# Feed forward's table preparation as single VectorE operations between attention's own, and the attention output copied ahead of the next tokens

## The chip, the cores and the metric

One core of a Trainium2 chip runs the program. The metric is the device time of one execution in microseconds (us); three executions were timed before the change, and one more was profiled.

## The reference, cut to what matters

Two layers on x (16 batches of 64 tokens of 512) with a context of the same shape. The change touches the end of the first layer's attention and the start of its feed forward:

```python
x = x + L0_xattn(_layernorm(x), ctx, Wq, Wk, Wv, Wo, q_norm_w, k_norm_w)   # 32 heads, 8 kv heads of 128
x = x + L0_ffn(_layernorm(x), gate_*, up_*, down_*)                        # 4 bit weights, inner size 1376
x = x + L1_xattn(ctx, _layernorm(x), ctx)
x = x + L1_ffn(_layernorm(x), W_org, lora_down, lora_up, lora_keys, Wq)

def _dequant(qweight, scales, qzeros, g_idx):
    w = (qw[:, None, :] >> shifts & 15).reshape(-1, N)
    z = ((qz[:, :, None] >> shifts & 15) + 1).reshape(groups, -1)
    return (w - z[g_idx]) * scales[g_idx]
h = silu(xf @ Wg) * (xf @ Wu);  out = h @ Wd
```

## The kernel before

**Attention** is cut into 64 units: 8 kv heads times 8 pairs of batches. The program of each engine is written out by hand as steps j = 0 to 67 (`pe_step0`, `act_step0`, `dve_step0`, `pool_step0`), and a step holds different stages of up to five units. On TensorE (PE), step j holds the query projection of unit j (L366), the transposes of unit j-1's normed queries and keys (L392, L395), the key and value projection of unit j (L378), the scores of unit j-1 (L406), the transposes of unit j-2's probabilities (L413), the output projection of unit j-3 (L423) and unit j-2's probabilities times values (L433). Every fp32 product is made of three with the operands split into a high part (copied by ScalarE, ACT) and a low part (subtracted by VectorE, DVE).

DVE's step has a fixed order: low part of unit j-3's attention output (`aoT`, L557), the sum of unit j-4's output into `acc` (L562), low part of unit j-1's values (`vv`, L566), then of unit j the sum of squares of the queries (L571), `msq` (L573), and, when GpSimd (POOL) has raised it to the power -0.5 (`rms`, L662), the normed queries (`qn`, L576). The same for the keys follows (L580, L582, POOL L665, L596), with unit j-1's score maximum (L586) and unit j-2's low part of the transposed probabilities (L590) between them, and at the end unit j-1's softmax division (L601, L603). PE's key and value projection of step j waits for `vv` of unit j-1, because both use the same PSUM bank.

**Feed forward's preparation** hangs behind the steps: after step j each engine runs `pe_ahead(j)`, `act_ahead(j)`, `dve_ahead(j)` or `pool_ahead(j)`, which do something from step 57 on (n = j - 56 in the code). DVE there takes the 4 bit zero points apart (L1046, 16 instructions behind steps 57 and 58), writes the zero table (L1058, behind step 59), and makes the one-hot tables of the group indices (`one_hot`, L1028 to L1034, behind steps 60 to 63), then the layer norm's statistics and tokens (L673 to L677, L685). ACT and POOL split the scale table into three bf16 parts (ACT L956 behind steps 57 to 62, POOL L763 behind steps 58 to 61). `spread` (PE, L848 and L853) multiplies one-hot by table, and `dequant` (DVE, L1096 to L1106) makes a piece of weights of it, which ACT (`w_hi`, L978) and POOL (`w_lo`, L776) split. `x2_hi` (ACT, L971) and `x2_lo` (DVE, L1164) split the transposed tokens (PE L933). The first product of feed forward is L874. SP's queue issues the loads, each in order behind its waits. No scheduler changes any of this: the engines run what the code has in the order it has, and wait on semaphores.

Of the kernel before, what the change touches and what calls it, by code (L numbers as in the profile page):

```python
# [17 lines left out]
ALU = mybir.AluOpType  # L18
# [40 lines left out]
def block_kernel(nc, a, out, stop=None):  # L59
# [27 lines left out]
    with root:  # L87
# [295 lines left out]
        def pe_step0(st):  # L383
# [15 lines left out]
            if st.has(1, UNITS):  # L399
# [111 lines left out]
        def act_step0(st):  # L511
            act = nc.scalar
            if st.has(3, UNITS):
# [3 lines left out]
                               ACT.Copy).then_inc(s_aohi, 1)  # L517
            if st.has(1, UNITS):
# [34 lines left out]
        def dve_step0(st):  # L553
# [9 lines left out]
            if st.has(1, UNITS):  # L563
# [3 lines left out]
                                  vv[:, par, HI, :, :].bitcast(F32), ALU.subtract).then_inc(s_vlo, 1)  # L567
            if st.has(0, UNITS):
# [4 lines left out]
                dve.tensor_scalar(msq[:, 0:4], ssq[:, 0:4], 1.0 / HD, RMS_EPS, ALU.mult, ALU.add).then_inc(s_qms, 1)  # L573
                dve.wait_ge(s_rq, st.done(0))
# [147 lines left out]
        def sp_ffn(sp):  # L722
# [8 lines left out]
            sp.wait_ge(s_zero_v, 18)  # L731
# [79 lines left out]
        def pe_ahead(j):  # L811
            pe = nc.tensor
            n = j - UNITS
            if n == 0:
# [4 lines left out]
                pe.wait_ge(s_idx_v, 8)  # L819
                pe.wait_ge(s_scale_v, 6)  # L820
                pe.wait_ge(s_zero_v, 18)
                pe.wait_ge(s_qn, UNITS)
                pe.wait_ge(s_vlo, UNITS)
                spread(pe, 0, (0, 1))
# [117 lines left out]
        def act_ahead(j):  # L942
# [76 lines left out]
        def one_hot(dve, part):  # L1019
# [3 lines left out]
                           (slice(2 * D, 2 * D + F), GD, oh_d[:, :]))[part // 2]  # L1023
            raw, n = idx_raw[:, cols], idx_n[:, 0:cols.stop - cols.start]
            if part:
                dve.wait_ge(s_idx_v, 2 * part)
            if part % 2 == 0:
                dve.tensor_scalar(n, raw, 0.0, float(g), ALU.is_lt, ALU.mult).then_inc(s_idx_v, 1)  # L1028
                dve.wait_ge(s_idx_v, 2 * part + 1)
                dve.tensor_tensor(n, raw, n, ALU.add).then_inc(s_idx_v, 1)  # L1030
            else:
                dve.tensor_scalar(n, n, float(g - 1), 0.0, ALU.min, ALU.max).then_inc(s_idx_v, 1)
                dve.wait_ge(s_idx_v, 2 * part + 1)
# [3 lines left out]

        def dve_ahead(j):
            dve = nc.vector
            n = j - EVEN_DONE  # L1040
            if n == 1 or n == 2:
                if n == 1:
                    dve.wait_ge(s_zraw, 48)
                for k in range(4 * (n - 1), 4 * n):
                    for g, lo, hi in ZERO_TABLES:
                        dve.tensor_scalar(z_int[0:g, lo // 8:hi // 8, k], z_raw[0:g, lo // 8:hi // 8], 4 * k, 15,  # L1046
                                          ALU.logical_shift_right, ALU.bitwise_and).then_inc(s_zero_v, 1)
            if n == 2:
                dve.wait_ge(s_pid, 1)
                dve.tensor_scalar(shift[:, :], pid[:, :], 7, 2, ALU.bitwise_and, ALU.logical_shift_left).then_inc(s_col, 1)  # L1050
                dve.tensor_scalar(grp_i[:, :], pid[:, :], 31, None, ALU.bitwise_and).then_inc(s_col, 1)
                dve.wait_ge(s_col, 2)
                dve.tensor_copy(grp[:, :], grp_i[:, :]).then_inc(s_col, 1)
            if n == 3:
                dve.wait_ge(s_zero_v, 16)
                dve.wait_ge(s_zero, 2)
                for g, lo, hi in ZERO_TABLES:
# [945 lines left out]
```

## Time and profile before

| | us |
|---|---|
| median of three executions | 1195.75 |
| lowest and highest | 1193.85 and 1198.1 |
| profiled execution | 1194.14 |
| its span, first to last instruction | 1192.3 |
| PE busy | 1124.5 (94% of the span) |
| DVE busy | 753.9 (63%) |
| ACT busy | 542.5 (46%) |
| POOL busy | 416.8 (35%) |

Times in a view are microseconds from the span's start. An engine's idle time before an instruction is given with what ended it: `[2.08 <-DVE vv L566]`. A timeline's row gives the start, the duration, the engine, the line, what is written and read, and how many instructions it stands for. An instruction's duration reaches a little into the next one of its engine, so the distance from start to start is shorter than the duration.

### The profile page before, as it was taken

Reading aid. Unit: us, or ns where it says so; the run is one execution under the profiler, and the core shown is the slowest. Engines: PE = TensorE matmul, PEld = TensorE weight load, DVE = VectorE, ACT = ScalarE, POOL = GpSimd, SP = SyncE. Lnnn points to the kernel's source line nnn. Section 1 sums busy time; section 2 is a strip of 40 time slices with the busy share of each in tenths; the row PEclk is TensorE's granted clock in tenths of the full one; section 3 lists DMA queues with packets and bytes.
Section 4 is the critical chain, followed back from the end, with each engine's and each line's share of the span. In section 5 each row is a group of like instructions: output and inputs, shape, how many; then the busy total and the mean of one; then the engine's idle time right before and its main releaser. Section 6 shows DMA issues by size and latency. Waiting matters only on the chain. (4 is left out here: it accounts for less than half of the span.)

```text
span 1192.3 us, 19230 instructions
## 1 busy us (share of the span) xinstructions
PE 1124.5 (94%) x6643; PEld 961.4 (81%) x6643; DVE 753.9 (63%) x1572; ACT 542.5 (46%) x1437; POOL 416.8 (35%) x421
## 2 busy tenths in 40 slices
PE   4899999999999999999999988799999999798998
PEld 3799999899899899999989887567777777676776
DVE  6555555555555555555555777889864666687863
ACT  4444454554544544544444545333323445454531
POOL 4443323323332232332332433144422324554531
PEclk9999999999999999999999999989999999898999
DMA  6211011111101101101100110122202245133300
GB/s 211 76 36 32 23 37 32 29 32 31 35 25 32 37 23 32 36 24 31 37 23 4 40 30 1 27 72 80 76 26 54 62 107 124 44 77 74 89 2 36
DMA packets 48716, 56.49 MB, mean 47 GB/s; under 512 B 10822, under 2 KB 29270, under 8 KB 48620
## 3 DMA queue, kind: packets, MB, share of 16 engines
q1 hardware_dynamic: 48620, 55.26, 17.2%
q8 instruction: 54, 0.88, 0.3%
q14 instruction: 42, 0.34, 0.1%
HBM read 40.56 MB, written 2.10 MB: 36 GB/s over the span
## 5 line engine op out<-in xcount | busy, mean ns | idle before, releaser
L378 PE MATMUL bank<-wqkv,kvT 128*128 128x256 f32 x1536 | 199.8, 286 | 8.7 <-DVE vv L566 8.7
L423 PE MATMUL bank<-wo,aoT 128*128 128x512 f32 x768 | 192.0, 399 | 5.7 <-DVE acc L562 5.7
L378 PEld LDWEIGHTS bank<-wqkv,kvT 128*128 128x128 f32 x1536 | 188.0, 192 | 10.4 <-DVE vv L566 10.4
L366 PE MATMUL bank<-wqkv,kvT 128*128 128x512 f32 x768 | 188.5, 395 | 1.7 <-DVE qn L576 1.7
L423 PEld LDWEIGHTS bank<-wo,aoT 128*128 128x128 f32 x768 | 139.5, 188 | 33.4 <-DVE aoT L557 6.3
L366 PEld LDWEIGHTS bank<-wqkv,kvT 128*128 128x128 f32 x768 | 141.5, 190 | 28.8 <-issue 1.8
L662 POOL TENSOR_TENSOR rms<-msq,half_neg 128x4 f32<-128x4 f32 x64 | 64.5, 1008 | 220.4 <-DVE msq L573 220.2
L874 PE MATMUL bank<-x2T,wgu 128*128 128x512 f32 (+1 forms) x336 | 91.5, 416 | 0.0
L549 ACT ACTIVATE prob<-bank,nmax 128x128 f32<-128x128 f32 x256 | 90.3, 372 | 2.1 <-DVE nmax L586 2.1
L1905 POOL TENSOR_TENSOR pr<-pr,rc 128x512 f32<-128x512 f32 x64 | 66.7, 1045 | 69.6 <-DVE rc L1774 69.5
L665 POOL TENSOR_TENSOR rms<-msq,half_neg 128x2 f32<-128x2 f32 x64 | 44.6, 697 | 132.0 <-DVE msq L582 132.0
L576 DVE TENSOR_TENSOR qn<-bank,rms 128x512 f32<-128x512 f32 x64 | 44.3, 692 | 71.7 <-POOL rms L662 71.7
L527 ACT ACTIVATE qsq<-bank 128x512 f32<-128x512 f32 x64 | 38.2, 597 | 112.8 <-PE bank L366 112.8
L557 DVE TENSOR_TENSOR aoT<-bank,aoT 128x512 fp32r<-128x512 f32 x64 | 44.2, 691 | 65.7 <-ACT aoT L516 65.7
L538 ACT ACTIVATE ksq<-bank 128x256 f32<-128x256 f32 x64 | 24.6, 384 | 131.8 <-PE bank L378 131.8
L571 DVE TENSOR_REDUCE ssq<-qsq 128x4 f32<-128x512 f32 x64 | 44.0, 687 | 63.9 <-ACT qsq L527 63.8
L470 POOL TENSOR_TENSOR wqkv<-wqkv_raw,wqkv 128x768 fp32r<-128x768 f32 x28 | 51.8, 1851 | 62.6 <-ACT wqkv L457 62.6
L874 PEld LDWEIGHTS bank<-x2T,wgu 128*128 128x128 f32 (+1 forms) x336 | 62.1, 192 | 13.3
L406 PE MATMUL bank<-kT,qT 128*128 128x128 f32 x512 | 67.6, 275 | 1.2 <-ACT qT L531 1.2
L895 PE MATMUL bank<-wd,hT 128*128 128x512 f32 (+1 forms) x264 | 68.6, 405 | 0.0
L543 ACT ACTIVATE pT<-bank 128x512 fp32r<-128x512 f32 x64 | 38.3, 599 | 60.4 <-PE bank L413 60.4
L1661 ACT ACTIVATE pmT<-bank 128x512 fp32r<-128x512 f32 x64 | 38.2, 597 | 59.5 <-PE bank L1440 59.3
(176 smaller groups left out, 2207.0 us busy)
## 6 DMA issues: line engine op xcount, KB each, us to landing
wqkv_raw<-in_L_xattn_Wq_dram SPq DMA_DIRECT2D x32, 256.0 KB, 2.5
wo_raw<-in_L_xattn_Wo_dram SPq DMA_DIRECT2D x32, 256.0 KB, 2.6
qS<-qhl SPq DMA_DIRECT2D x32, 256.0 KB, 3.7
kS<-chl SPq DMA_DIRECT2D x32, 128.0 KB, 3.0
packed<-_L_ffn_gate_qweight_dram SPq DMA_DIRECT2D x40, 64.0 KB, 2.4
packed<-in_L_ffn_up_qweight_dram SPq DMA_DIRECT2D x40, 64.0 KB, 2.3
packed<-_L_ffn_down_qweight_dram SPq DMA_DIRECT2D x10, 256.0 KB
acc<-in_x_dram SPq DMA_DIRECT2D x8, 256.0 KB, 5.7
```

The costliest lines, as they stand in the source:

```text
L366: mm = pe.matmul(b_q[:, :], kvT[:, l, kt, p, 1:3, :], wqkv[:, par, r, kt, 0:QW], start=(kt == 0 and n == 0), stop=(kt == KT - 1 and n == 2))
L378: mm = pe.matmul(b_kv[:, b * 256:(b + 1) * 256], kvT[:, l, kt, p, 2 * b:2 * b + 2, :], wqkv[:, par, r, kt, QW:QKV], start=(kt == 0 and n = ...
L406: mm = pe.matmul(b_s[:, n * P:(n + 1) * P], qT[:, b, 2 * hp:2 * hp + 2, :], kT[:, b, :], start=True, stop=True)
L423: mm = pe.matmul(b_o[:, :], aoT[:, l, h, :, :], wo[:, par, r, h, :], start=(h == 0 and n == 0), stop=(h == G - 1 and n == 2))
L470: pool.tensor_tensor(wqkv[:, par, LO, n, :], wqkv_raw[:, n % 2, :], wqkv[:, par, HI, n, :].bitcast(F32), ALU.subtract).then_inc(s_wqkv, 1)
L549: act.activation(prob[:, n, :], b_s[:, n * P:(n + 1) * P], ACT.Exp, bias=nmax[:, n:n + 1], accum_out=psum_row[:, n:n + 1]).then_inc(s_exp, 1)
L576: dve.tensor_tensor(qn[:, :, :], b_q[:, :].rearrange("p (h d) -> p h d", h=G), rms[:, 0:4].unsqueeze(2).to_broadcast([P, G, HD]), ALU.mult ...
L662: pool.tensor_tensor(rms[:, 0:4], msq[:, 0:4], half_neg[:, 0:4], ALU.pow).then_inc(s_rq, 1)
L665: pool.tensor_tensor(rms[:, 4:6], msq[:, 4:6], half_neg[:, 4:6], ALU.pow).then_inc(s_rk, 1)
L874: mm = pe.matmul(b[0:w, :], wgu[:, f, l, m, kt, 0:w], x2T[:, r, kt, :], start=(kt == 0 and k == 0), stop=(kt == KT - 1 and k == 2))
L895: mm = pe.matmul(f_d[t][:, :], hT[0:w, l, t * P:(t + 1) * P], wd[0:w, f, r, :], start=(f == 0 and k == 0), stop=(f == FT - 1 and k == 2))
L1905: pool.tensor_tensor(pr[:, t % PT_, :], pr[:, t % PT_, :], rc1[:, t % 4:t % 4 + 1].to_broadcast([P, D]), ALU.mult).then_inc(s_n1, 1)
```

## The change

Every DVE piece of the table preparation that stood behind a step becomes single operations at three places of a step: "q" (behind `vv`, ahead of the queries' sum of squares), "rq" (behind `msq`, ahead of `qn`, while POOL makes `rms`) and "end" (behind the step, as before, but with one piece and not all). The zero table is written in three instructions and not two, so the semaphore's count is 19. The first `spread` moves on PE from behind step 64 into it. ACT's copies of the feed forward's tokens move from behind steps 64 and 65 to behind the `aoT` copy of steps 65 and 66. DVE makes the first two pieces of weights behind step 64 and not behind step 65, and ahead of the `x2_lo` of the first two token tiles.

```diff
@@ pe_step0, behind the scores
+            if st.j == UNITS:
+                pe.wait_ge(s_idx_v, 8)
+                pe.wait_ge(s_scale_v, 6)
+                pe.wait_ge(s_zero_v, 19)
+                pe.wait_ge(s_qn, UNITS)
+                pe.wait_ge(s_vlo, UNITS)
+                spread(pe, 0, (0, 1))
@@ act_step0, behind the aoT copy
+            act_tokens2(act, st.j - UNITS)
@@ dve_step0
+            dve_between(dve, st.j, "q")
             if st.has(0, UNITS):
...
                 dve.tensor_scalar(msq[:, 0:4], ssq[:, 0:4], 1.0 / HD, RMS_EPS, ALU.mult, ALU.add).then_inc(s_qms, 1)
+                dve_between(dve, st.j, "rq")
                 dve.wait_ge(s_rq, st.done(0))
@@ sp_ffn
-            sp.wait_ge(s_zero_v, 18)
+            sp.wait_ge(s_zero_v, 19)
@@ pe_ahead, n == 0
-                pe.wait_ge(s_idx_v, 8)
...
-                spread(pe, 0, (0, 1))
@@ act_ahead
-            if n == 8:
-                x2_hi(act, 0)
-                x2_hi(act, 1)
             if n == 9:
-                x2_hi(act, 2)
-                x2_hi(act, 3)
                 w_hi(act, 0, (0, 1))
+        def act_tokens2(act, n):
+            if n == 1 or n == 2:
+                x2_hi(act, 2 * n - 2)
+                x2_hi(act, 2 * n - 1)
@@ dve_ahead
+        BETWEEN = {(1, "q"): (0,), (1, "rq"): (1,), (1, "end"): (2,),
+                   (2, "q"): (3,), (2, "rq"): (4,), (2, "end"): (5,),
+                   (3, "q"): (6,), (3, "rq"): (7,), (3, "end"): ("columns",),
+                   (4, "q"): ("gate",), (4, "rq"): ("up",), (4, "end"): ("down",)}
+        HOT = {(5, "q"): (0,), (5, "rq"): (1,), (5, "end"): (2,),
+               (6, "q"): (3,), (6, "rq"): (4,), (6, "end"): (5,),
+               (7, "q"): (6,), (7, "rq"): (7,)}
...
-            if n == 9 or n == 10:
-                for p in (2 * (n - 9), 2 * (n - 9) + 1):
+            if n == 8:
+                dequant(dve, 0, (0, 1))
+            if n == 9:
+                for p in (0, 1):
                     dve.wait_ge(s_x2hi, p + 1)
                     x2_lo(dve, p)
-            if n == 9 or n == 10:
-                dequant(dve, 0, (2 * (n - 9), 2 * (n - 9) + 1))
+            if n == 10:
+                for p in (2, 3):
+                    dve.wait_ge(s_x2hi, p + 1)
+                    x2_lo(dve, p)
+                dequant(dve, 0, (2, 3))
```

Number k in the first table is a nibble position (two instructions, L1046 before), in the second one of the eight one-hot operations: 0 to 3 make `oh_gu` (1024 columns), 4 to 7 `oh_d` (1376 columns).

DVE from step 60's last operation to step 62's first, before the change; `idx_n` and `oh_gu` are the one-hot work:

```order
L603 TENSOR_TENSOR prob<-prob,rsum 128x512
L1028 TENSOR_SCALAR idx_n<-idx_raw 128x1024
L1030 TENSOR_TENSOR idx_n<-idx_raw,idx_n 128x1024
L673 BN_STATS stat<-acc 128x6
L675 BN_AGGR mv<-stat 128x2
L677 TENSOR_SCALAR mv<-mv 128x1
L557 TENSOR_TENSOR aoT<-bank,aoT 128x512
L562 TENSOR_TENSOR acc<-bank,acc 128x512
L566 TENSOR_TENSOR vv<-bank,vv 128x256
L571 TENSOR_REDUCE ssq<-qsq 128x4
L573 TENSOR_SCALAR msq<-ssq 128x4
L576 TENSOR_TENSOR qn<-bank,rms 128x512
```

and now (the lines have moved: L565 is before's L557, L586 its L576, L1032 its L1028):

```order
L613 TENSOR_TENSOR prob<-prob,rsum 128x512
L1061 TENSOR_SCALAR zs<-z_int 10x512
L683 BN_STATS stat<-acc 128x6
L685 BN_AGGR mv<-stat 128x2
L687 TENSOR_SCALAR mv<-mv 128x1
L565 TENSOR_TENSOR aoT<-bank,aoT 128x512
L570 TENSOR_TENSOR acc<-bank,acc 128x512
L574 TENSOR_TENSOR vv<-bank,vv 128x256
L1032 TENSOR_SCALAR idx_n<-idx_raw 128x1024
L580 TENSOR_REDUCE ssq<-qsq 128x4
L582 TENSOR_SCALAR msq<-ssq 128x4
L1034 TENSOR_TENSOR idx_n<-idx_raw,idx_n 128x1024
```

Two one-hot operations have left the stretch between `prob` and `aoT` for the two places around the sum of squares; the last part of the zero table has come into it.

ACT from step 64's exponentials to the first copies of weights, before:

```order
L549 ACTIVATE prob,psum_row<-bank,nmax 128x128 x3
L971 ACTIVATE x2T<-bank 128x4x128 [waits s_tx2] x2
L516 ACTIVATE aoT<-bank 128x512 [waits s_o,s_pv]
L543 ACTIVATE pT<-bank 128x512 [waits s_pv,s_pt]
L971 ACTIVATE x2T<-bank 128x4x128 [waits s_tx2] x2
L978 ACTIVATE wgu<-wtmp 128x256 [waits s_wt] x2
L516 ACTIVATE aoT<-bank 128x512 [waits s_o,s_pv]
```

and now:

```order
L557 ACTIVATE prob,psum_row<-bank,nmax 128x128 x3
L523 ACTIVATE aoT<-bank 128x512 [waits s_o,s_pv]
L975 ACTIVATE x2T<-bank 128x4x128 [waits s_tx2] x2
L551 ACTIVATE pT<-bank 128x512 [waits s_pv,s_pt]
L982 ACTIVATE wgu<-wtmp 128x256 [waits s_wt] x2
L523 ACTIVATE aoT<-bank 128x512 [waits s_o,s_pv]
L975 ACTIVATE x2T<-bank 128x4x128 [waits s_tx2] x2
```

Both copies of the attention output (`aoT`) have passed the pair of token copies (`x2T`) that stood ahead of them.

DVE in the same steps, from step 64's `prob` to step 65's `acc`, now:

```order
L613 TENSOR_TENSOR prob<-prob,rsum 128x512 [waits s_rec]
L1127 TENSOR_SCALAR nib<-packed,shift 128x256 [waits s_packed0]
L1133 TENSOR_TENSOR wint<-nib,bank 128x256 [waits s_zs,s_nib]
L1137 TENSOR_TENSOR wtmp<-wint,bank 128x256 [waits s_nib]
L1127 TENSOR_SCALAR nib<-packed,shift 128x256 [waits s_nib]
L1133 TENSOR_TENSOR wint<-nib,bank 128x256 [waits s_wt,s_zs,s_nib]
L1137 TENSOR_TENSOR wtmp<-wint,bank 128x256 [waits s_nib]
L683 BN_STATS stat<-acc 128x6 [waits s_acc]
L685 BN_AGGR mv<-stat 128x2 [waits s_bn]
L687 TENSOR_SCALAR mv<-mv 128x1 [waits s_bn]
L565 TENSOR_TENSOR aoT<-bank,aoT 128x512 [waits s_aohi]
L570 TENSOR_TENSOR acc<-bank,acc 128x512 [waits s_o]
```

The six instructions of `dequant` (L1127 to L1137) stood a step later before, behind `x2_lo`; now they are ahead of step 65's `aoT`.

## Rows read from the trace of the kernel before

**Rows 1.** Windows by step, 57 and 59 to 63: width, then busy time of each engine

```profile
656.44:667.52 11.08, 11.08 (x75) 10.04 (x74) 6.60 (x14) 5.33 (x16) 2.38 (x3) 1.00 0.01 1
...
679.96:692.43 12.47, 11.34 (x74) 10.06 (x73) 9.49 (x25) 6.24 (x17) 5.14 (x5) 1.00 0.30 100
692.43:704.82 12.39, 11.35 (x75) 10.07 (x74) 9.43 (x16) 6.49 (x17) 5.13 (x5) 1.00 0.24 64
704.82:718.24 13.42, 11.34 (x75) 10.06 (x74) 10.37 (x19) 6.48 (x17) 5.14 (x5) 1.00 0.01 1
718.24:731.18 12.94, 11.34 (x74) 10.06 (x73) 9.88 (x20) 6.48 (x17) 4.06 (x5) 1.00 0.01 2
731.18:744.09 12.91, 11.35 (x74) 10.07 (x73) 9.85 (x20) 5.24 (x16) 2.23 (x3) 1.00 0.00 0
```

**Rows 2.** Timeline of PE: the key and value projection of steps 57 and 61

```profile
659.76 3.12 PE L378 MATMUL bank<-wqkv,kvT 128*128 128x256 f32 x24
...
710.47 3.13 PE L378 MATMUL bank<-wqkv,kvT 128*128 128x256 f32 x24 [2.08 <-DVE vv L566]
```

**Rows 3.** Timeline of DVE: the idle places in step 57

```profile
660.02 0.69 DVE L571 TENSOR_REDUCE ssq<-qsq 128x4 f32<-128x512 f32 x1 [1.13 <-ACT qsq L527]
...
662.03 0.69 DVE L576 TENSOR_TENSOR qn<-bank,rms 128x512 f32<-128x512 f32 x1 [1.12 <-POOL rms L662]
663.33 0.42 DVE L580 TENSOR_REDUCE ssq<-ksq 128x2 f32<-128x256 f32 x1 [0.61 <-ACT ksq L538]
```

**Rows 4.** Timelines of POOL, then DVE: the end of step 60, the start of 61

```profile
702.00 3.46 POOL L763 TENSOR_TENSOR s_raw<-s_raw,zs 128x816 f32<-128x816 f32 x2
...
703.79 2.22 DVE L603 TENSOR_TENSOR prob<-prob,rsum 128x512 f32<-128x512 f32 x1
705.94 0.68 DVE L1028 TENSOR_SCALAR idx_n<-idx_raw 128x1024 f32<-128x1024 int32 x1
...
707.79 0.69 DVE L673 BATCH_NORM_STATS2 stat<-acc 128x6 f32<-128x512 f32 x1
...
708.80 0.68 DVE L557 TENSOR_TENSOR aoT<-bank,aoT 128x512 fp32r<-128x512 f32 x1
```

**Rows 5.** Timelines of ACT and DVE: the start of step 58

```profile
668.42 1.57 ACT L956 ACTIVATE zs<-s_raw 128x1632 bf16<-128x1632 f32 x1 [1.66 <-issue]
...
670.50 0.69 DVE L557 TENSOR_TENSOR aoT<-bank,aoT 128x512 fp32r<-128x512 f32 x1 [0.46 <-ACT aoT L516]
```

**Rows 6.** Table work: two lines' durations (ns, least/median/most), one row of the timeline

```profile
L1030 DVE TENSOR_TENSOR idx_n<-idx_raw,idx_n x2: 1226/1410/1593, 706.6 to 731.7; 128x1024 f32<-128x1024 int32 x1, 128x1376 f32<-128x1376 int32 x1
...
681.08 1.75 DVE L1046 TENSOR_SCALAR z_int<-z_raw 4x344 int32<-4x344 int32 x8
...
L1058 DVE TENSOR_SCALAR zs<-z_int x2: 408/991/1574, 693.5 to 695.0; 4x2752 bf16<-4x2752 int32 x1, 10x512 bf16<-10x512 int32 x1
```

**Rows 7.** A POOL power beside a DVE operation, and that line's durations (ns)

```profile
8.81 0.54 DVE L685 TENSOR_SCALAR xn<-acc,mv,rstd 128x512 f32<-128x512 f32 x1
...
8.97 0.79 POOL L681 TENSOR_TENSOR rstd<-mv,half_neg 128x1 f32<-128x1 f32 x1 [2.59 <-DVE mv L677]
...
L681 POOL TENSOR_TENSOR rstd<-mv,half_neg x24: 543/552/1235, 5.8 to 1167.9; 128x1 f32<-128x1 f32 x24
```

**Rows 8.** Timeline of all engines, steps 65 and 66

```profile
754.12 0.69 DVE L557 TENSOR_TENSOR aoT<-bank,aoT 128x512 fp32r<-128x512 f32 x1 [1.53 <-ACT aoT L516]
...
758.03 0.34 DVE L1096 TENSOR_SCALAR nib<-packed,shift 128x256 int32<-128x256 int32 x1
...
758.38 0.87 PE L433 MATMUL bank<-pT,vv 128*128 128x256 f32 x6
...
760.38 0.69 DVE L673 BATCH_NORM_STATS2 stat<-acc 128x6 f32<-128x512 f32 x1
...
761.31 0.60 ACT L516 ACTIVATE aoT<-bank 128x512 fp32r<-128x512 f32 x1
...
763.38 2.98 PE L423 MATMUL bank<-wo,aoT 128*128 128x512 f32 x12 [3.25 <-DVE acc L562]
```

More of the change, by code:

```diff
@@ L1017, in hidden_hi, with one_hot @@
             act.activation(hT[0:w, HI, :], hval[0:w, :], ACT.Copy).then_inc(s_hhi, 1)
[L1019 removed]
+        def one_hot(dve, k):
             cols, g, to = ((slice(0, 2 * D), GG, oh_gu[:, :, :].rearrange("p m k -> p (m k)")),
[L1023 removed]
+                           (slice(2 * D, 2 * D + F), GD, oh_d[:, :]))[k // 4]
             raw, n = idx_raw[:, cols], idx_n[:, 0:cols.stop - cols.start]
[L1025 to L1027 removed]
+            if k:
+                dve.wait_ge(s_idx_v, k)
+            if k % 4 == 0:
@@ L1034, in one_hot, with zero_bits @@
                 dve.tensor_scalar(to, n, grp[:, 0:1], None, ALU.is_equal).then_inc(s_idx_v, 1)
         ZERO_TABLES = ((GG, GATE, UP + F), (GD, DOWN, DOWN + D))
+        def zero_bits(dve, k):
+            if k == 0:
+                dve.wait_ge(s_zraw, 48)
+            for g, lo, hi in ZERO_TABLES:
+                dve.tensor_scalar(z_int[0:g, lo // 8:hi // 8, k], z_raw[0:g, lo // 8:hi // 8], 4 * k, 15,
+                                  ALU.logical_shift_right, ALU.bitwise_and).then_inc(s_zero_v, 1)
@@ new lines, in columns, with zero_table @@
+        def columns(dve):
+            dve.wait_ge(s_pid, 1)
+            dve.tensor_scalar(shift[:, :], pid[:, :], 7, 2, ALU.bitwise_and, ALU.logical_shift_left).then_inc(s_col, 1)
+            dve.tensor_scalar(grp_i[:, :], pid[:, :], 31, None, ALU.bitwise_and).then_inc(s_col, 1)
+            dve.wait_ge(s_col, 2)
+            dve.tensor_copy(grp[:, :], grp_i[:, :]).then_inc(s_col, 1)
+        def zero_table(dve, k):
+            if k == 0:
+                dve.wait_ge(s_zero_v, 16)
+                dve.wait_ge(s_zero, 2)
+            g, lo, hi = ((GG, GATE, UP), (GG, UP, UP + F), (GD, DOWN, DOWN + D))[k]
+            dve.tensor_scalar(zs[0:g, 0, lo:hi], z_int[0:g, lo // 8:hi // 8, :].rearrange("p c j -> p (c j)"), 1, None,
+                              ALU.add).then_inc(s_zero_v, 1)
@@ new lines, in block_kernel, with dve_between @@
+        BETWEEN = {(1, "q"): (0,), (1, "rq"): (1,), (1, "end"): (2,),
[3 rows of a table added]
+        HOT = {(5, "q"): (0,), (5, "rq"): (1,), (5, "end"): (2,),
+               (6, "q"): (3,), (6, "rq"): (4,), (6, "end"): (5,),
+               (7, "q"): (6,), (7, "rq"): (7,)}
+        def dve_between(dve, j, where):
+            n = j - EVEN_DONE
+            for k in BETWEEN.get((n, where), ()):
+                if k == "columns":
+                    columns(dve)
+                elif k in ("gate", "up", "down"):
+                    zero_table(dve, ("gate", "up", "down").index(k))
+                else:
+                    zero_bits(dve, k)
+            for k in HOT.get((n, where), ()):
+                if k == 0:
+                    dve.wait_ge(s_col, 3)
+                    dve.wait_ge(s_idx, 48)
+                one_hot(dve, k)
@@ L1040, in dve_ahead @@
             n = j - EVEN_DONE
[L1041 to L1057, printed above, removed]
-                    dve.tensor_scalar(zs[0:g, 0, lo:hi], z_int[0:g, lo // 8:hi // 8, :].rearrange("p c j -> p (c j)"), 1, None,
-                                      ALU.add).then_inc(s_zero_v, 1)
-            if n == 4:
-                dve.wait_ge(s_col, 3)
-                dve.wait_ge(s_idx, 48)
-            if 4 <= n <= 7:
-                one_hot(dve, n - 4)
+            dve_between(dve, j, "end")
             if n == 6 or n == 7:
-                dve.wait_ge(s_zero_v, 18)
+                dve.wait_ge(s_zero_v, 19)
                 ln_apply(dve, X2, n - 6, xn2[:, n - 6, :])
```

10 lines of the change are left out of this document (3 added, 7 removed).

## The prediction

> **What bounds the kernel now.** First the windows cut at the starts of the query projection, one per step [rows 1]: the first number is the step's width, then comes each engine's busy time. Step 57, the last in which DVE does attention's work alone, takes 11.08 us and PE is busy through all of it, so attention is bound by PE. Steps 59 to 63 take 12.47, 12.39, 13.42, 12.94 and 12.91 with the same PE work: 1.39, 1.31, 2.34, 1.86 and 1.83 us too long, 8.73 in all. Next the idle time of PE inside such a step: it is all in one place, ahead of the key and value projection, and ended by DVE's `vv` [rows 2]. Undisturbed, that projection starts 3.32 after the step (659.76 less 656.44).
>
> DVE's last four rows around a step's boundary tell why [rows 4]. Behind `prob` stand the table operations and the statistics, and only then `aoT`, which opens the next step. From `aoT` to PE's projection it takes 710.47 less 708.80, 1.67. So `aoT` may start 1.65 after the step's start (3.32 less 1.67) and PE loses nothing; in step 61 it started 3.98 after it (708.80 less 704.82), which gives the loss of 2.33.
>
> The same DVE sits idle elsewhere in a step [rows 3]: 1.13 ahead of the queries' sum of squares, 1.12 ahead of `qn` while POOL makes `rms`, 0.61 ahead of the keys' sum. The change moves work from the boundary, where it costs, to the first two of these.
>
> **Step 58 stays as it is.** It has a stall too, but there DVE waited for ACT's `aoT` copy [rows 5], and that stood behind ACT's 1.57 us `zs` copy, which did not start before 668.42. Nothing of that is moved: saved 0.
>
> **Steps 59 and 60.** At the end of steps 58 to 61 POOL subtracts in the scale table for 3.46 us, and `prob`, which has no more elements than DVE's 0.69 us rows [rows 3], takes 2.22 because it is held until POOL's second instruction ends [rows 4]. The operation behind it then starts 1.12 after the next step's start (705.94 less 704.82). The change leaves that hold alone. Eight nibble instructions took 1.75 [rows 6], so a pair takes 0.44. Behind step 58 one pair is left: `aoT` at 1.56, below 1.65. Behind step 59 three one-column instructions are left, estimated at no more than a pair. Both stalls go: 1.39 and 1.31 saved. The margin is 0.09; what is late next, if it doesn't hold, is PE's projection by as much as the pair is longer. The pairs at "q" and "rq" (0.44 each) are covered by the idle 1.13 and 1.12; without that cover they would cost 0.44 each.
>
> **Step 61.** In step 60 the two gate and up tables stand at "q" and "rq", each half of the 1.57 us instruction [rows 6], some 0.8; both fit their idle places. At the end are left the down table (0.41, 0.34 from start to start) and the statistics (707.79 to 708.80, 1.01). `aoT` starts at 1.12 + 0.34 + 1.01 = 2.47, PE's projection at 4.14, a stall of 0.82 in place of 2.34: 1.52 saved.
>
> **Step 62.** Left at step 61's end are one one-hot operation, as long as L1028 (0.68, taken as 0.71 with the step to the next), and the statistics: `aoT` at 2.84, a stall of 1.19. But step 61 itself is now full. `aoT` stands at 2.47, the sum of squares could follow 1.54 later (just before `vv` ends), "q" adds 0.71, and "rq" holds L1030, 1.23 us, all SBUF to SBUF. Beside what POOL does that matters. The nearest row is a power that began 0.16 behind a DVE operation of 0.54 and took 0.79, where the line's median is 0.55 [rows 7]: 0.24 longer, with the DVE operation 0.38 into it. So POOL loses the overlap less 0.14. For L1030 that is 1.07 less 0.14, 0.93. The bounds are 0 and the whole 1.07; I take 0.93, by the row. Then `qn` starts 2.01 behind the sum (662.03 less 660.02) plus 0.93, and the keys' sum 0.69 behind that: 2.47 + 1.54 + 0.71 + 2.01 + 0.93 + 0.69 = 8.35. PE's projection lets it start at 4.14 + 3.57 (663.33 less 659.76) = 7.71. It is 0.64 late, POOL's keys' power and its 3.46 us of subtractions are 0.64 late with it, and so is the release of `prob`. The stall becomes 1.19 + 0.64 = 1.83: 0.03 saved, 0.67 if nothing is late.
>
> The Trainium skill (SBUF: State Buffer, Who interferes with whom) says that DVE and GpSimd share one port pair, and that whichever comes first holds it for its whole instruction. By that rule the power would lose all of 1.07, and the sum below would be 0.14 smaller; the row has 0.24 where the rule has 0.38, so I stay with the row.
>
> **Step 63.** POOL subtracts nothing behind step 62. One operation on 1376 columns leaves that boundary (0.68 times 1376/1024, estimated at 0.91), L1030's long form (1.59) stays. Step 62 is full in the same way, but its "rq" operation is shorter, and by the same working some 0.1 late. 0.8 saved of 1.83.
>
> **Steps 64 to 66.** Here three moves meet [rows 8]. (a) Two one-hot operations leave the end of step 63; what PE needs next waits mostly for ACT, so I count only some 0.4 of earlier work in DVE's step 64. (b) Two pieces of weights, 758.03 to 760.38, 2.35 us, now stand ahead of step 65's `aoT`. That one was idle for 1.53 before 754.12 (for ACT's copy), so DVE was free at 752.59; with 2.35 more and 0.4 less it starts at 754.5, 0.4 later than before, and the output projection with it. Bounds: 0.8 later, or not at all. (c) ACT's copy of the last unit's `aoT` no longer waits behind two token copies and two weight copies. It was made at 761.31 though what it reads was complete at 758.38 + 0.87; it can start at 759.3, with (b) at 759.7. From it to the last output projection it took 2.07, so that starts at 761.8 and not at 763.38: 1.6 saved, (b) already off it. DVE is free in time: it has 2.35 less to do in step 65. Behind that projection come `spread`, `dequant` and the first products in the same order as before, and SP's loads are released by the same instructions, earlier. The whole shift therefore passes on to the end. PE's moved `spread` is the same work in another place of the same step.
>
> **Sum.** 1.39 + 1.31 + 1.52 + 0.03 + 0.8 + 1.6 = 6.65 us. Against the profiled execution, 1194.14, that gives 1187.5. The median of the runs shown is 1.6 above it, and gives 1189.1. I forecast the middle, **1188.3**; 0.3% (3.6 us) is what the measurement can tell.
>
> **Rivals.**
> 1. *POOL's powers suffer more than by the row.* If an "rq" operation delays the keys' chain in steps 60 to 63 by a further 0.6 each, half of steps 61 and 63 is given back. Gain 6.65 less 2.0: 1190.3. For it: one row alone prices the overlap. Against: steps 60, 62 and 63 have shorter operations there. 0.14.
> 2. *Issue order turns at the hold.* `prob` starts 0.06 behind POOL's second subtraction (702.00 + 3.46/2 is 703.73). In steps 60 and 61 POOL's chain is delayed, by up to 0.64, `prob` by less, since the exponentials have some slack. Then DVE is first. If it keeps POOL out until its boundary work is done, the operation behind `prob` starts at -0.42 (703.79 + 0.61 less 704.82) and not at 1.12: step 61's stall of 0.82 and step 62's 1.83 go nearly whole. Gain 9.2: 1185.7. Against: POOL may come in between `prob` and the next operation, and nothing is won. The skill's page above gives the pair to whoever starts first, which is this rival's first half. 0.12.
> 3. *ACT is the real bound.* ACT's 1.57 copies stand ahead of its `aoT` copy behind every step to 62, as in step 58. If steps 59 and 60 fall back on it, 2.7 stays and the gain is 4: 1191. Against: in step 61 DVE ran from `prob` into `aoT` without a pause [rows 4], and in step 58 it was idle [rows 5]. With (c) or (b) failing as well, it ends within 0.3%. 0.06, and 0.05 for that joint case.
> 4. *Slower: the gaps aren't free.* DVE's idle at "q" and "rq" is a wait for ACT and POOL. If each operation there pushes what follows by its whole length (POOL and DVE holding each other), six pairs (2.6), two tables (1.6) and five one-hot operations (some 4.7) come onto the path, 8.9, beside the 2.9 that the boundaries still cost, against 8.73 now; with 0.8 from (b) and nothing from (c) that is 3.9 more: 1198.0. It decides from the point where a delay exceeds 1.1 at an idle place in every one of steps 57 to 63; the idle places of 1.13 and 1.12 stand against it. 0.03.
>
> **Numbers.** The forecast has 0.60. The range 1184.8 to 1191.8 takes in rivals 1 to 3, and the spread of the runs shown (4.25) about the sum. Faster by over 0.3%: 0.89 (the forecast, rivals 1, 2 and most of 3). Within 0.3%: 0.08. Slower: 0.03.
>
> **What would show it.** Windows by step after: step 58 about 12.4; 59 and 60 at 11.1; 61 about 11.9; 62 about 12.9; 63 about 12.1; DVE's L603 still at 2.2 four times; POOL's L662 longer in steps 61 to 63 than in the steps before; ACT's last `aoT` copy straight behind the probabilities' product. It is wrong if steps 59 and 60 still show PE idle for `vv`, if step 62 is down to 11.1 (rival 2), or if the last output projection starts no sooner behind step 64's start than 19.3 (763.38 less 744.09).

## The result, and the profile after

| | before | after |
|---|---|---|
| median, us (lowest to highest, executions) | 1196.87 (1193.85 to 1198.1, 4) | 1185.52 (1184.88 to 1188.28, 4) |
| profiled execution | 1194.14 | 1188.28 |
| its span | 1192.3 | 1186.5 |

The ratio (of the means) is 0.9913 with the interval 0.9887 to 0.9939: faster by 0.9%, and inside the forecast's range. A second set of the same kernel gave 1185.79 (0.9921, 0.9905 to 0.9937). It has more executions, 6 and 23, so those numbers are the firmer ones.

The windows by step of the changed kernel, 57 to 63 (width, then PE, PE's weight loads, DVE, ACT, POOL busy, clock, DMA share, GB/s), answer to [rows 1]:

```profile
656.01:667.09 11.08, 11.08 (x74) 10.04 (x73) 7.51 (x18) 5.32 (x16) 2.41 (x3) 1.00 0.01 1
667.09:679.52 12.43, 11.35 (x75) 10.07 (x73) 8.63 (x19) 7.33 (x17) 8.41 (x7) 1.00 0.00 1
679.52:690.60 11.08, 11.08 (x75) 10.04 (x73) 9.03 (x20) 6.24 (x17) 5.17 (x5) 1.00 0.37 112
690.60:701.68 11.08, 11.08 (x75) 10.04 (x73) 9.35 (x19) 6.48 (x17) 5.68 (x5) 1.00 0.01 2
701.68:713.58 11.90, 11.35 (x75) 10.07 (x73) 10.22 (x21) 6.36 (x17) 5.68 (x5) 1.00 0.25 66
713.58:726.00 12.42, 11.35 (x75) 10.06 (x73) 10.74 (x20) 6.71 (x17) 5.24 (x5) 1.00 0.01 2
726.00:737.99 11.99, 11.35 (x75) 10.07 (x73) 10.37 (x21) 5.33 (x16) 2.85 (x3) 1.00 0.00 0
```

From step 57's start to step 64's it takes 81.98 (737.99 less 656.01) in place of 87.65 (744.09 less 656.44): 5.67 less. The profiled executions differ by 5.86 in all, and of that 0.43 had come before step 57 (656.44 less 656.01), where the change touches nothing. Steps 59 and 60 have lost their stall. What is left stands ahead of the same projection as before, as PE's timeline of the changed kernel shows for steps 58, 61, 62 and 63 (answering to [rows 2]), and, for the tail, the last two output projections (to [rows 8]):

```profile
671.74 3.14 PE L378 MATMUL bank<-wqkv,kvT 128*128 128x256 f32 x24 [1.08 <-DVE vv L574]
...
705.80 3.14 PE L378 MATMUL bank<-wqkv,kvT 128*128 128x256 f32 x24 [0.55 <-DVE vv L574]
...
718.22 3.14 PE L378 MATMUL bank<-wqkv,kvT 128*128 128x256 f32 x24 [1.07 <-DVE vv L574]
...
730.21 3.14 PE L378 MATMUL bank<-wqkv,kvT 128*128 128x256 f32 x24 [0.64 <-DVE vv L574]
...
749.67 4.58 PE L430 MATMUL bank<-wo,aoT 128*128 128x512 f32 x12 [2.87 <-DVE acc L570]
754.09 0.87 PE L440 MATMUL bank<-pT,vv 128*128 128x256 f32 x6
754.81 1.03 PE L937 MATMUL bank<-ident,xn 128*128 128x128 f32 x8
757.07 2.96 PE L430 MATMUL bank<-wo,aoT 128*128 128x512 f32 x12 [1.23 <-DVE acc L570]
```

"Behind S64" means from here on: from the start of step 64. Step 65's output projection takes 4.58 for the same 12 matmuls that take 2.96 in the last row. TensorE's granted clock was half, the lower of its two levels, from 750.5 to 753.9 in this profile. That is where the tail's gain went: the last output projection starts 19.08 behind step 64's start (757.07 less 737.99), and 19.29 before (763.38 less 744.09). DVE's `aoT` of step 65 and ACT's copy of the last unit's `aoT`, from two timelines:

```profile
748.25 0.68 DVE L565 TENSOR_TENSOR aoT<-bank,aoT 128x512 fp32r<-128x512 f32 x1
...
755.00 0.60 ACT L523 ACTIVATE aoT<-bank 128x512 fp32r<-128x512 f32 x1 [6.81 <-PE bank L440]
```

DVE around the end of step 61, and POOL beside it, show what the overlaps did (to [rows 4] and [rows 7]):

```profile
706.26 0.68 DVE L580 TENSOR_REDUCE ssq<-qsq 128x4 f32<-128x512 f32 x1
...
707.05 1.22 DVE L1034 TENSOR_TENSOR idx_n<-idx_raw,idx_n 128x1024 f32<-128x1024 int32 x1
709.17 0.69 DVE L586 TENSOR_TENSOR qn<-bank,rms 128x512 f32<-128x512 f32 x1 [0.90 <-POOL rms L672]
709.78 0.41 DVE L590 TENSOR_REDUCE ssq<-ksq 128x2 f32<-128x256 f32 x1
...
712.78 0.69 DVE L613 TENSOR_TENSOR prob<-prob,rsum 128x512 f32<-128x512 f32 x1
713.39 2.24 DVE L1036 TENSOR_SCALAR idx_n<-idx_n 128x1024 f32<-128x1024 f32 x1
715.55 0.68 DVE L683 BATCH_NORM_STATS2 stat<-acc 128x6 f32<-128x512 f32 x1
```

```profile
684.07 1.04 POOL L672 TENSOR_TENSOR rms<-msq,half_neg 128x4 f32<-128x4 f32 x1 [3.90 <-DVE msq L582]
...
707.22 1.91 POOL L672 TENSOR_TENSOR rms<-msq,half_neg 128x4 f32<-128x4 f32 x1 [4.89 <-DVE msq L582]
...
711.13 3.95 POOL L773 TENSOR_TENSOR s_raw<-s_raw,zs 128x816 f32<-128x816 f32 x2
```

The power beside the 1.22 us operation took 1.91. In step 59, beside a pair of short nibble instructions, the same took 1.04. POOL's two subtractions of step 61 took 3.95 together, and 3.46 before [rows 4].

### The profile page after: what moved, and what is told of

It reads as the page before. It is cut to its first block and busy times, and to the rows that moved or that the text cites. A ratio compares the mean times of both kernels' runs of the same rounds, so it can differ in the third digit from the quotient of the medians.

```text
span 1186.5 us, 19231 instructions
## 1 busy us (share of the span) xinstructions
PE 1127.2 (95%) x6643; PEld 964.1 (81%) x6643; DVE 754.4 (64%) x1573; ACT 542.2 (46%) x1437; POOL 417.6 (35%) x421
## 5 line engine op out<-in xcount | busy, mean ns | idle before, releaser
L672 POOL TENSOR_TENSOR rms<-msq,half_neg 128x4 f32<-128x4 f32 x64 | 67.1, 1049 | 219.4 <-DVE msq L582 219.1
L557 ACT ACTIVATE prob<-bank,nmax 128x128 f32<-128x128 f32 x256 | 90.1, 371 | 1.4 <-DVE nmax L596 1.3
L586 DVE TENSOR_TENSOR qn<-bank,rms 128x512 f32<-128x512 f32 x64 | 44.2, 691 | 69.4 <-POOL rms L672 69.4
L565 DVE TENSOR_TENSOR aoT<-bank,aoT 128x512 fp32r<-128x512 f32 x64 | 44.1, 690 | 67.8 <-ACT aoT L523 67.8
```

The source lines that it names most:

```text
L557: act.activation(prob[:, n, :], b_s[:, n * P:(n + 1) * P], ACT.Exp, bias=nmax[:, n:n + 1], accum_out=psum_row[:, n:n + 1]).then_inc(s_exp, 1)
L672: pool.tensor_tensor(rms[:, 0:4], msq[:, 0:4], half_neg[:, 0:4], ALU.pow).then_inc(s_rq, 1)
```

## The experiments

Each kernel ran on one chip together with executions of the kernel before; "S64" is read as in the windows above. The readings to be told apart were these. In the steps: DVE's boundary work behind POOL's hold is the bound, or ACT's copies are. In the tail: ACT's copy order is what held the last projection, and the two pieces of weights that DVE makes early are what the clock's fall comes from.

**The changed kernel again.**

> The changed kernel once more, for more times and a second profile. Theory A (two gains: some 5.6 us from the shorter steps 59 to 63, 1.6 us from the last output projection, which the first profile hid because PE ran at half clock under step 65's output projection): step widths as in the first profile (61 at 11.9, 62 at 12.4, 63 at 12.0), and if the clock is full there, the last output projection starts 17.5 to 17.8 us behind the start of step 64 and not 19.1. Time 6 to 9 us below before. Theory B (the tail gains nothing, the dequantisation ahead of aoT eats it): that distance stays at 19 or more at full clock too, and the time is 5 to 6 us below before.

Measured: 1185.79 (1184.38 to 1186.36, 6 executions), the kernel before in the same set 1195.18 (1191.19 to 1198.89, 23). The widths of the steps agree with the first profile within 0.03, the last output projection starts 19.09 behind S64, and the clock is half again from 748.7 to 752.2, at the same place of the program. So neither the rest of the stalls nor the fall is an accident of one execution.

**The kernel before again.**

> The kernel before, submitted as if it were a change. It shows what the comparison gives for no change (both theories: ratio 1.000 within 0.002) and, in its profile, where the half clock stretches fall in another execution: if they fall at other places and the span differs by 1 to 4 us, the spread of the times of one kernel (1193.85 to 1198.1) is the clock's.

Measured: ratio 1.0003 (0.9991 to 1.0015). The profile, though, differs from the first at two places. PE's timeline in step 61, then the window of that step, then PE's timeline at the last output projection:

```profile
710.93 4.63 PE L378 MATMUL bank<-wqkv,kvT 128*128 128x256 f32 x24 [2.09 <-DVE vv L566]
```

```profile
705.27:720.20 14.93, 12.84 (x75) 11.55 (x74) 10.39 (x19) 6.50 (x17) 5.15 (x5) 0.89 0.00 1
```

```profile
765.30 4.58 PE L423 MATMUL bank<-wo,aoT 128*128 128x512 f32 x12 [3.25 <-DVE acc L562]
```

The stall in step 61 is the same, 2.09 for 2.08, but behind it the clock is half from 711.2 to 714.6, and the step takes 14.93 where it took 13.42. In this execution steps 57 to 63 cost 1.51 more than in the one that the prediction was summed against; the next kernel, which has the same steps, shows it too. And the last output projection, which took 2.98 behind the same idle time of 3.25 [rows 8], took 4.58 here.

**The tail's moves alone**: PE's `spread`, ACT's token copies and DVE's early weights as in the change, the tables behind the steps as before.

```diff
 (the kernel before, and of the change:)
+            if st.j == UNITS:
...
+                spread(pe, 0, (0, 1))
+            act_tokens2(act, st.j - UNITS)
+            if n == 8:
+                dequant(dve, 0, (0, 1))
```

> Only the moves of steps 64 to 66 (spread in the step, aoT copied ahead of the tokens, first dequantisation ahead of step 65); the tables stand as before. Theory A: steps 58 to 63 as before (12.4, 12.5, 12.4, 13.4, 12.9, 12.9), the last output projection some 17.7 us behind the start of step 64 and not 19.3, time 1.6 us below before. Theory B: that distance at 19 or more, time as before within 0.5 us.

Measured: 1195.7, ratio 1.0 (0.9989 to 1.0012). PE's timeline of this kernel:

```profile
750.11 0.60 PE L850 MATMUL bank<-zs,oh_gu 128*128 128x256 bf16 x4 [1.41 <-DVE vv L574]
...
758.82 5.46 PE L430 MATMUL bank<-wo,aoT 128*128 128x512 f32 x12 [2.87 <-DVE acc L570]
```

`spread` now stands inside the step, ahead of work that doesn't need it, and waits 1.41 for DVE's `vv`, since DVE's one-hot work still stands behind step 63: the step's output projection is at 5.35 behind S64 (4.23 before). Then the 2.87 of idle time and the half clock follow, as in the whole change, and the last projection is at 21.91 (17.7 was expected if the tail's moves gained, 19 or more if they did not). By themselves the tail's moves gain nothing. That the time is unchanged although the last projection is 2.62 later shows too that its start alone doesn't give the time.

**The tables alone**: DVE's single operations, everything else as before.

```diff
 (the changed kernel, undoing:)
-            if st.j == UNITS:
...
-                spread(pe, 0, (0, 1))
-            act_tokens2(act, st.j - UNITS)
-            if n == 8:
-                dequant(dve, 0, (0, 1))
```

> Only the table operations at q, rq and end; spread, the token copies, the first dequantisation and x2_lo stand as before the change. Theory A: steps 59 to 63 as in the changed kernel (11.1, 11.1, 11.9, 12.4, 12.0), 5.5 us below before, and the last output projection 19.0 to 19.3 us behind the start of step 64. Theory B: the same, but no slower than the whole change.

Measured: 1186.78 (1186.15 to 1188.38), ratio 0.9933 (0.9917 to 0.995), in one set with the three above: the tables carry nearly all of the gain, and their time isn't told apart from the whole change's. The widths of steps 58 to 63 are those of the changed kernel within 0.02. In the tail the output projections stand at 3.35, 10.61 and 18.42 behind S64 (4.23, 11.47, 19.29 before), so the emptier boundary behind step 63 is worth some 0.87 there, and no projection is at half clock.

**The changed kernel without DVE's early weights.**

```diff
-            if n == 8:
-                dequant(dve, 0, (0, 1))
...
+            if n == 9 or n == 10:
+                for p in (2 * (n - 9), 2 * (n - 9) + 1):
+                    dve.wait_ge(s_x2hi, p + 1)
+                    x2_lo(dve, p)
+            if n == 9 or n == 10:
+                dequant(dve, 0, (2 * (n - 9), 2 * (n - 9) + 1))
```

> The change without its DVE move in steps 64 to 66: the first dequantisation and x2_lo stand where they stood before; tables, spread and the aoT copies are the change's. Theory C (the dequantisation ahead of step 65's aoT lengthens PE's idle time ahead of that output projection to 2.9 us, and the clock falls under it, which ate the tail's gain): step 65's output projection starts 9 to 9.6 us behind the start of step 64 and not 11.7, takes 2.98 us and not 4.58, the last one starts at 16.5 to 17.3 and not 19.1; time 1.5 to 3 us below the whole change. Theory D (the fall has nothing to do with the idle time; it comes at that place or any other): the first number falls as in C, but that projection still takes over 4 us in the profile, or the time stays as the whole change's.

PE's timeline of this kernel:

```profile
747.17 3.00 PE L430 MATMUL bank<-wo,aoT 128*128 128x512 f32 x12 [0.79 <-DVE acc L570]
...
754.74 2.99 PE L430 MATMUL bank<-wo,aoT 128*128 128x512 f32 x12 [2.99 <-DVE acc L570]
```

With S64 at 737.57 the projections of steps 65 and 66 are at 9.60 and 17.17. The idle time ahead of step 65's is 0.79 and not 2.87, it runs at full clock, and the last starts 1.91 earlier than in the changed kernel. The time is 1185.61 (1183.55 to 1185.83), ratio 0.9908 (0.9892 to 0.9923), which is not told apart from the whole change; 1.5 to 3 less was expected. The 1.91 is there in the trace and not in the median: behind it feed forward has stretches at half clock of its own, at other places in each profile (in this one from 769.9 to 776.8, in the changed kernel from 767.6 to 771.0, 774.4 to 777.8 and 876.8 to 880.2).

**ACT's `zs` copies behind its `vv` copy of the next step**, everything else as changed.

```diff
 (act_step0, behind the copy of vv)
+            act_scale(act, st.j - 1 - EVEN_DONE)
 (act_ahead)
-        def act_ahead(j):
...
+        def act_scale(act, n):
```

> The change with ACT's six scale table copies moved from ahead of the aoT copy to behind the vv copy of the same step, into ACT's idle time. My reading of step 58 (its stall is ACT's, not DVE's): step 58 falls from 12.4 to 11.1 us, the other steps stay, time 1.3 us below the whole change. The rival (DVE's nibble pair held by POOL until 668.7 is the bound there): step 58 stays above 12.

Step 58 goes from 12.43 to 11.09 wide and the other steps stay within 0.02: ACT's copy was step 58's bound, and no other step's. The time is 1186.83 (1181.87 to 1187.95), ratio 0.9916 (0.9899 to 0.9933). That doesn't show the 1.34; here the half clock in the tail lasted from 748.3 to 755.2, twice as long, and the last projection stood at 20.28 behind S64, 1.20 later than in the changed kernel.

**POOL's two subtractions apart**: one behind its power of the queries, the other behind the step.

```diff
                 pool.tensor_tensor(rms[:, 0:4], msq[:, 0:4], half_neg[:, 0:4], ALU.pow).then_inc(s_rq, 1)
+                if 2 <= st.j - EVEN_DONE <= 5:
+                    scale_rest(pool, st.j - EVEN_DONE, 0)
...
-                for q in (2 * half, 2 * half + 1):
...
+                scale_rest(pool, n, 1)
```

> The change with POOL's two subtractions of a step taken apart: the first behind the queries' power, the second behind the keys' power as now. If POOL's hold of prob (1.5 us) is what still lengthens steps 61 and 62: L613 is down from 2.23 to 0.7 to 1.1 in four steps, the operation behind it is not held either, step 61 falls from 11.9 to 11.1 and step 62 from 12.4 to 11.1 to 11.6, and the time is 1.5 to 2 us below the whole change. If the first subtraction only delays the keys' power and all behind it, the steps stay within 0.3 us of the change's.

Steps 61 and 62 are 11.08 and 11.17 wide (11.90 and 12.42 as changed), and step 63 stays at 12.00. `prob` takes 0.69 in every step. POOL's second subtraction, queued behind the first, was what held DVE at the boundary. Of the 2.07 gained the tail took 1.2 back, at half clock from 746.8 to 753.6 and with the last projection at 20.31 behind S64; the expected 1.5 to 2 less of time didn't come: 1185.37 (1184.6 to 1187.05), ratio 0.9912 (0.9896 to 0.9927).

**The last three together** (DVE's early weights back, ACT's late `zs` copies, POOL's subtractions apart). The edits are those above.

> All three together. If they are independent: steps 58 to 62 at 11.1 to 11.5, 63 at about 12, the last output projection 16.5 to 17.3 us behind the start of step 64, and a time 4.5 to 6 us below the whole change, near 1180.5.

The windows of steps 57 to 63, cut to the last four:

```profile
689.23:700.30 11.07, 11.07 (x74) 10.03 (x73) 8.26 (x16) 6.60 (x16) 5.69 (x4) 1.00 0.00 1
700.30:711.38 11.08, 11.08 (x74) 10.04 (x73) 9.08 (x19) 6.59 (x16) 6.42 (x5) 1.00 0.27 73
711.38:722.55 11.17, 11.17 (x74) 10.07 (x73) 9.49 (x21) 6.49 (x16) 3.63 (x4) 1.00 0.01 2
722.55:734.55 12.00, 11.36 (x75) 10.07 (x73) 10.37 (x21) 6.60 (x16) 2.85 (x3) 1.00 0.00 0
```

POOL and DVE at the end of step 61 of this kernel (two timelines):

```profile
708.59 0.70 POOL L678 TENSOR_TENSOR rms<-msq,half_neg 128x2 f32<-128x2 f32 x1
709.26 1.75 POOL L766 TENSOR_TENSOR s_raw<-s_raw,zs 128x816 f32<-128x816 f32 x1
```

```profile
710.89 0.69 DVE L614 TENSOR_TENSOR prob<-prob,rsum 128x512 f32<-128x512 f32 x1
711.50 0.69 DVE L1044 TENSOR_SCALAR idx_n<-idx_n 128x1024 f32<-128x1024 f32 x1
```

POOL's subtraction at the end of the step is all but over when `prob` starts (711.01 and 710.89), and both DVE operations take 0.69 where one of them took 2.2. Of the 8.73 us of stalls in steps 59 to 63 only step 63's 0.92 and 0.09 of step 62's are left, and step 58's is gone too. The last projection is at 17.15, at full clock. The time is 1183.14 (1180.7 to 1186.6), ratio 0.9893 (0.9874 to 0.9913). That is less of a gain than was expected (near 1180.5).

**The same with the table operations handed out anew**, so that step 63 has one and its boundary none.

```diff
+        BETWEEN = {(1, "q"): (0, 1), (1, "rq"): (2, 3), (1, "end"): (4,),
+                   (2, "q"): (5,), (2, "rq"): (6,), (2, "end"): (7,),
+                   (3, "q"): ("gate",), (3, "rq"): ("up",), (3, "end"): ("down",),
+                   (4, "q"): ("columns",)}
+        HOT = {(4, "q"): (0,), (4, "rq"): (1,), (4, "end"): (2,),
+               (5, "q"): (3,), (5, "rq"): (4,),
+               (6, "q"): (5,), (6, "rq"): (6,),
+               (7, "q"): (7,)}
```

> All three of the last run, and the table operations handed out anew: two nibble pairs at q and rq of step 57, everything else one to three places earlier, so that nothing but statistics and tokens stands behind steps 61 to 63, and the 1.59 us addition on 1376 columns at q of step 62. My reading (what lengthens step 63 is that addition behind step 62): step 63 falls from 12.0 to 11.1 to 11.4, steps 57 to 62 stay at 11.1 to 11.3, 0.7 to 0.9 us below the last run. Rival (the addition at q delays the queries' chain by as much): step 63 stays at 11.8 or more, or step 62's successor chain lengthens step 64.

The windows of steps 62 and 63:

```profile
711.85:722.93 11.08, 11.08 (x74) 10.04 (x73) 9.46 (x20) 6.59 (x16) 3.29 (x4) 1.00 0.01 2
722.93:734.01 11.08, 11.08 (x74) 10.04 (x73) 8.49 (x19) 6.47 (x16) 2.23 (x3) 1.00 0.00 0
```

All of steps 57 to 63 are now within 0.01 of PE's own 11.08, but for 0.06 in step 61. What had kept step 63 at 12.00 was the addition on 1376 columns behind step 62: at "q" of step 62 its 1.58 us cost that step nothing. The last projection, though, takes 4.35 in this profile, after 2.98 of idle time, where it took 2.99 after 2.99 in the kernel above. The time is 1183.29 (1181.6 to 1185.0), ratio 0.9889 (0.9872 to 0.9905): the last microsecond of stalls isn't told apart.

**The same with DVE's second piece of weights behind step 66's `aoT`.** What stands ahead of the last `aoT` is one piece now, not two.

```diff
             if n == 9:
...
+                dequant(dve, 0, (0,))
             if n == 10:
+                dequant(dve, 0, (1,))
                 for p in (2, 3):
...
-                w_hi(act, 0, (0, 1))
+                w_hi(act, 0, (0,))
...
-                w_hi(act, 0, (2, 3))
+                w_hi(act, 0, (1, 2, 3))
```

> The run before, with the second piece of the first dequantisation moved behind step 66's aoT and acc. If DVE's work ahead of step 66's aoT sets the last output projection (it starts 17.15 us behind the start of step 64, with PE idle for 2.99): it starts at 15.9 to 16.2, the first product of feed forward at 19.2 to 19.6 in place of 20.35. If the moved piece only comes onto feed forward's path instead: the last output projection is earlier by 1.2, the first product stays at 20.3.

The last projection starts at 16.01 behind S64 (17.19 in the kernel above). 1180.76 (1179.99 to 1181.89), ratio 0.9868 (0.9853 to 0.9884). PE's timeline has the clock's fall under that last projection this time, and so feed forward's first product starts at 20.79 where 19.2 to 19.6 was expected. With DVE's early weights gone the fall can still come, as in the kernel above and in the second profile of the kernel before.

```profile
750.76 4.58 PE L430 MATMUL bank<-wo,aoT 128*128 128x512 f32 x12 [1.85 <-DVE acc L571]
```

**The same with `spread` behind step 64, as in the kernel before.**

```diff
 (pe_step0)
-            if st.j == UNITS:
...
-                spread(pe, 0, (0, 1))
 (pe_ahead, n == 0)
+                spread(pe, 0, (0, 1))
```

> The run before, with the first spread back behind step 64 on PE, as it stood before the change. In the step it stands ahead of the output projection, which then starts 3.78 us behind the step's start; in the run with the tables alone it was 3.35. If that 0.43 is on the path: the first output projection at 3.35, step 65's 0.4 earlier than in the run before, and the time 0.4 us lower, which two medians cannot tell apart but the trace can. If DVE sets step 65's projection: only the first number moves.

PE's timeline, the three output projections behind S64 at 734.36:

```profile
737.70 3.01 PE L423 MATMUL bank<-wo,aoT 128*128 128x512 f32 x12
...
743.52 3.00 PE L423 MATMUL bank<-wo,aoT 128*128 128x512 f32 x12 [0.35 <-DVE acc L564]
...
750.21 2.98 PE L423 MATMUL bank<-wo,aoT 128*128 128x512 f32 x12 [2.10 <-DVE acc L564]
```

They start at 3.34, 9.16 and 15.85, all at full clock, and feed forward's first product at 19.04; `spread`'s 0.44 fills PE's gap ahead of the second. 1180.68 (1177.62 to 1182.28), ratio 0.9864 (0.9845 to 0.9883). In time that is the kernel above, although its first product came 1.75 earlier. The two are the fastest versions here, 0.9864 and 0.9868 of the kernel before in one set (1196.61), where the changed kernel was 0.9921 of it in another.

## Why the prediction was right, and where its terms were not

The forecast was 1188.3 with a gain of 6.65; the profiled executions differ by 5.86, the medians of the second set by 9.39 (1195.18 less 1185.79), and those of the first by 11.35. The measured gain is thus larger than the forecast one. Step by step:

- **Step 58, saved 0: right, and for the reason given.** Width 12.44 before, 12.43 after. Moving ACT's `zs` copies behind its `vv` copy, and nothing else, took the stall away.
- **Steps 59 and 60, 1.39 and 1.31: right.** Both are 11.08 wide. `aoT` was to start 1.56 behind step 59's start; it started at 1.53 (681.05 less 679.52).
- **Step 61, 1.52: right.** Width 11.90 for a predicted 11.9. Against executions like the second profile of the kernel before the gain here is 1.5 larger: no profile of a kernel with the new tables has the fall of the clock behind the stall, which is 0.55 now. No term of the sum had that.
- **Step 62, 0.03: mis-sized, it saved 0.52** (12.94 less 12.42). The first half of the working holds. L1030's operation (now L1034) delayed POOL's power by 0.90, for a predicted 0.93: from the queries' sum to `qn` it takes 2.91 (709.17 less 706.26) where it took 2.01 [rows 3]. What failed is the end, and in two places. The release was to be 0.64 late with the keys' chain; POOL's subtractions started 9.45 behind the step (711.13 less 701.68), where 8.26 in step 60 of the same profile plus the stall of 0.82 makes 9.08: they were 0.37 late. And `prob`, that is held "until POOL's second instruction ends" in the prediction, was not held. In this step DVE was first. `prob` took 0.69, POOL's second subtraction came in behind it, and DVE's next operation was held, 2.24 in place of 0.69. Rival 2 had that turn of the order, and had beside it as the argument against that POOL may come in between and nothing is won. So it went: the hold only moved on by one operation, and that operation's own 0.7 was now inside it. POOL's end came later for it, since the pair took 3.95 and not 3.46. The stall became 1.32 (718.22 less 713.58, less 3.32) rather than 1.83.
- **Step 63, 0.8: 0.92** (12.91 less 11.99). Right within 0.12.
- **Steps 64 to 66, 1.6: wrong, it was 0.21** (19.29 less 19.08), just inside the prediction's own sign of being wrong, which was 19.3. Each link of the order was as told. DVE's `aoT` of step 65 came 0.23 later behind S64 than before (748.25 less 737.99 is 10.26; 754.12 less 744.09 is 10.03), for a predicted 0.4. ACT's last copy started as soon as PE's product was complete, and from it to the last projection it took 2.07 (757.07 less 755.00), the predicted 2.07. What failed is what stood between, taken at full clock: step 65's projection took 4.58 rather than 2.98. The last one was to start 17.71 behind S64 (761.8 less 744.09) and was 1.37 later; the half clock alone makes 1.60, and small shifts 0.23 the other way. Term (b) was costed by the delay of `aoT` only. The other effect is that PE's idle time ahead of the projection is 2.87 and no longer 1.77: PE starts it 0.21 later behind S64, and is ready for it 0.89 earlier, since step 63 leaves less behind and `spread` has moved. The emptier boundary itself, (a), was put at 0.4 and is worth 0.87 with the tables alone; the moved `spread`, taken as free, put step 64's projection at 3.78 rather than 3.35. With DVE's weights back in their old place that idle time is 0.79, the clock stays up, and the last projection starts at 17.17, where the prediction's own steps give 17.3 without (b) (759.3 plus 2.07 less 744.09). That the early weights bring the fall at this place is shown by that kernel; that they do it through the longer idle time is the likely way, and is not shown apart from it.
- **Behind the tail, "the whole shift passes on to the end": not shown.** From S64 to the end of the first feed forward's down products it takes 276.46 after and 275.52 before, 0.94 more, although the last projection is 0.21 earlier; the changed kernel's extra stretches at half clock lie in between. The second profiles have 276.45 after and 277.42 before, so even the sign changes with the execution of the kernel before. The kernel without the early weights started its last projection 1.91 earlier and didn't show it in the median either.

**The sum.** The median is 2.8 below the forecast, in the range's lower part. Against the profiled execution the terms came out 0.8 too large together: the tail gave 1.4 less, step 62 0.5 more. That the medians differ by more than the profiles do is partly the kernel before. It loses a further 1.51 wherever the clock falls in step 61, which the profiled execution that the sum was made against didn't show, and two later profiles with the old steps did. So what the tail's term had too much, 1.4, is about what step 61's lacked in such executions: that the number stayed in the range owes something to luck. How often the clock falls there isn't settled by three profiles, and the other 2 us between 5.86 and 9.39 are left open. What the profiles do show is that parts that no edit touches differ by that much. The start of step 57 lies between 654.45 and 657.12 in the 13 profiles. And behind feed forward's down products the second layer starts at half clock for different lengths (1020.2 to 1033.8 in the first profile of the changed kernel, 1018.4 to 1028.6 in the second).

**The rivals.** Rival 1 fell: the powers lost what the row priced. Rival 2 came true in its first half, in step 61, and brought almost nothing of its 9.2. Rival 3 fell: of ACT's copies only step 58's mattered. Rival 4 fell with steps 59 and 60 at PE's own 11.08.

**The rule of the Trainium skill.** Its page "SBUF — State Buffer", section "Who interferes with whom", says that whichever of DVE and GpSimd comes first holds the shared port pair for its whole instruction, while the other is blocked. `prob` in steps 58 to 60 and L1036 in step 61 agree with it, 2.2 for a row of 0.69 while POOL's second subtraction runs. The power beside L1034 started 0.17 into the 1.22 us operation and lost 0.90, where the rule gives 1.05; so, as in [rows 7], the loss is some 0.15 less than the overlap. Step 62's power, begun 0.17 into an operation of 0.87, took 1.56 for 1.01, the same 0.15 less.

## What to carry to other kernels

Look for the place where the bound engine waits, and move the helper's work to where the helper itself idles; here the idle places of steps 59 and 60 took single operations of up to 0.86 us for nothing, the 1.22 us one in step 61 made POOL's chain 0.37 late, and in a later kernel one of 1.58 us behind `vv` was free. Two long instructions of GpSimd back to back were worse for VectorE here than the same two apart, since the queued second one held the VectorE operation at the step's end, 2.2 us in place of 0.69. And a stall's length isn't its price: cost the work behind it at the lower clock as well (here 1.5 to 1.6 us more, 2.5 in three profiles), and look at more than one execution of the kernel before, since the clock fell in one and not in the next.

## What the runs showed of the hardware, beyond the expected

- **A gap alone doesn't tell whether TensorE's clock falls.** Ahead of step 65's projection 2.87 to 2.92 of idle time were followed by half clock in each of the five profiles that have DVE's early weights (the changed kernel twice, the tail alone, the late `zs`, the split subtractions), and its 12 matmuls took 4.58 or 5.46. In the eight profiles without them the idle time there is 0.35 to 1.77, and they took 2.96 to 3.01. Ahead of the last projection it is mixed. 3.25 was followed by full clock in one profile of the kernel before and with the tables alone, and by half clock in the other profile of the kernel before (4.58); 2.98 to 2.99 by full clock in two kernels and by a fall in a third (4.35); 1.85 by half clock; 2.10 by full clock. In the five profiles where the clock had just fallen at step 65 the last projection was at full clock. In step 61 the same 2.1 was followed by half clock in one profile of the kernel before and in that of the tail alone, and by full clock in the other. What sets it wasn't found.
- **DVE and POOL took turns instruction by instruction.** When DVE came first at the hold (712.78 here, and the same in the second profile), it did not keep POOL out for the operations that it had ready: POOL's queued instruction was next, and DVE's second one took 2.24.
- **Some work was free.** In step 57 DVE's busy time rose from 6.60 to 7.51, and the step stayed at 11.08. Steps 59 and 60 came down to 11.08 with 9.03 and 9.35 of busy time, of which some 1.5 each is `prob` being held.
